# Attention on one Trainium2 core: four scores and two maxima tiles in one stretch a step, weighted sums one step behind

## What is computed

```python
scores = jnp.einsum('bqhd,bkhd->bhqk', Q, K) / np.sqrt(HEAD_DIM)      # 16 wide heads
scores = scores + slopes[None, :, None, None] * rel[None, None, :, :]
attn = jax.nn.softmax(scores, axis=-1)
out = jnp.einsum('bhqk,bkhd->bqhd', attn, V).reshape(bsz, seq_len, EMBED_DIM)
```

## Time and profile before

| | us |
|---|---|
| time before, median of 3 runs | 5108.2 |
| lowest and highest of the runs | 5095.89 and 5113.9 |
| span of the profiled execution | 5138.9 |
| of it the attention's loop, from the trace | 337 to 2909 |
| PE, DVE, ACT busy in that loop | 2556.23, 2502.93, 2248.42 |

### The profile page before, as it was taken

How to read it: one execution, slowest core, us unless ns; L and a number is a source line. 1 busy time by engine, 2 the same in 40 slices (tenths; PEclk the granted TensorE clock), 3 DMA queues, 4 the chain that set the end, 5 groups by cost and what they waited for, 6 DMA issues and landing times. The chain is left out here.

```text
span 5138.9 us, 109366 instructions
## 1 busy us (share of the span) xinstructions
PE 4706.1 (92%) x35413; PEld 2589.8 (50%) x35413; DVE 4275.5 (83%) x6882; ACT 3471.8 (68%) x6677; POOL 1377.0 (27%) x1279
## 2 busy tenths in 40 slices
PE   5869999999999999999999689999599999955998
PEld 4723333333333333333333267777366666645887
DVE  5779999999999999999999768878677877775554
ACT  2428888888888888888888523223377877734554
POOL 1111111111111111111111133333234443435776
PEclk8969999999999999999999889999699999956999
DMA  4931222212222122221222211111100000044442
GB/s 153 349 67 35 52 52 46 43 35 53 52 46 43 35 53 51 46 43 38 50 54 43 71 40 37 41 45 37 53 21 27 25 23 28 21 156 164 166 160 92
DMA packets 236717, 340.13 MB, mean 66 GB/s; under 512 B 60215, under 2 KB 170034, under 8 KB 227612
## 3 DMA queue, kind: packets, MB, share of 16 engines
q1 hardware_dynamic: 220032, 275.39, 22.3%
q0 software_dynamic: 16192, 58.43, 3.1%
HBM read 205.62 MB, written 136.18 MB: 67 GB/s over the span
## 5 line engine op out<-in xcount | busy, mean ns | idle before, releaser
L719 DVE TENSOR_REDUCE at_mxp<-at_ps_m 128x2 f32<-128x1024 f32 x2092 | 2524.4, 1221 | 70.2 <-PE at_ps_m L772 47.3
L692 ACT ACTIVATE at_prob<-at_ps_s 128x512 f32<-128x512 f32 x4100 | 2227.3, 596 | 323.5 <-PE at_ps_s L762 299.7
L782 PE MATMUL at_ps_o<-at_prob,at_vs 128*32 128x256 f32 x16384 | 1313.1, 392 | 13.9 <-ACT at_osum L698 13.9
L762 PE MATMUL at_ps_s<-at_qs,at_ks 51*128 51x512 f32 x4100 | 1036.7, 500 | 2.7 <-ACT at_prob L692 2.7
L772 PE MATMUL at_ps_m<-at_ks,at_qs 49*128 49x512 f32 x4184 | 859.0, 406 | 49.8 <-DMA at_ks<-t_alibi 34.4
L762 PEld LDWEIGHTS at_ps_s<-at_qs,at_ks 51*128 51x128 f32 x4100 | 384.6, 183 | 853.3 <-ACT at_prob L692 852.8
L782 PEld LDWEIGHTS at_ps_o<-at_prob,at_vs 128*32 128x32 f32 x16384 | 322.9, 108 | 778.2 <-issue 389.7
L564 POOL TENSOR_TENSOR at_total<-at_total,at_minus 128x16 f32<-128x16 f32 x65 | 189.6, 2917 | 1128.4 <-DMA at_total<-at_osum 1128.4
L772 PEld LDWEIGHTS at_ps_m<-at_ks,at_qs 49*128 49x128 f32 x4184 | 403.7, 190 | 73.7 <-DVE at_mxp L719 38.0
L67 DVE TENSOR_TENSOR ex_hidc<-ex_hid,ex_hidc 128x512 fp32r<-128x512 f32 x128 | 158.5, 1250 | 169.6 <-ACT ex_hid L2550 169.6
L1222 PE MATMUL mi_ps_f<-mi_w,mi_act 128*128 128x256 f32 x1024 | 260.1, 399 | 17.4 <-DVE mi_acc L1072 17.1
(11 more groups left out here) (317 smaller groups left out, 6161.6 us busy)
## 6 DMA issues: line engine op xcount, KB each, us to landing
t_parts<-pr_parts SPq DMA_DIRECT2D x64, 512.0 KB, 6.4
ex_w<-in_fw SPq DMA_DIRECT2D x32, 1024.0 KB, 7.4
at_ks<-t_parts SPq DMA_DIRECT2D x102, 256.0 KB
t_buf<-at_blank POOLq DMA_DIRECT2D x64, 384.5 KB, 3.2
at_qs<-t_parts SPq DMA_DIRECT2D x96, 256.0 KB
at_vs<-t_v SPq DMA_DIRECT2D x17, 1024.0 KB, 4.8
ex_rest<-t_buf SPq DMA_DIRECT2D x16, 1026.0 KB, 5.2
t_v<-pr_vaug SPq DMA_DIRECT2D x64, 256.0 KB, 5.6
```

The lines of the kernel that those rows point to most:

```text
L692: nc.scalar.activation(prob[0 if up is None else (t + 1) % 2][:, j, :], ps_s[bank][:, :], ACT.Exp).then_inc(s_read, 1)
L719: nc.vector.tensor_reduce(out[:, s4, k + i, 2 * pair:2 * pair + 2], ps_m[i][:, :, :], AX.X, ALU.max).then_inc(mx_read, 1)
L762: nc.tensor.matmul(ps_s[bank][:, :], ks[s][a:a + QROWS, j // 2, t1 * P:(t1 + 1) * P], qs[s][a:a + QROWS, j // 2, c * T:(c + 1) * T], start ...
L782: last = nc.tensor.matmul(ps_o[32 * j:32 * j + 32, q0:q1], vs[s][:, t, 32 * j:32 * j + 32], prob[t % 2][:, j, q0:q1], start=(t == 0 and ha ...
```

## The change

In the new order a step has one row-tiled stretch and one column-tiled stretch: scores 0 and 1, maxima tile 0, score 2, score 3, maxima tile 1, and then all four weighted sums at once, for all 512 queries, with the probabilities of the step before. The scores are shifted by one head: a chunk's step t holds heads 1, 2 and 3 of its own step and head 0 of the next (`head`). `at_prob` has four tiles in place of two. The copy of a chunk's sums moves behind the four exponentials of the next chunk's first step, and PE's waits for it and for the new values (`v_in`) to that chunk's second step; the wait for the next chunk's maxima moves from before score 0 of the last step to before its score 3. Before the loop one score stands in place of four, behind two more memsets on POOL (a slice of `at_vs` and one `at_prob` tile), and the first weighted sum works on those ones; behind the loop one weighted sum is added. The two matmuls of a maxima tile change places. The number of PSUM banks of the scores is still 3.

```diff
+        PROBS = 4
+        prob = [sb(f"prob{r}", [P, HPG, T]) for r in range(PROBS)]
...
+        AHEAD = RING + 1
...
             if up is None:
-                return j, bank_of(LOOP - HPG + j), 0
+                return 0, bank_of(LOOP - 1), 0
             back = next(a for a in range(1, LOOP) if bank_of((k - a) % LOOP) == bank_of(k))
-            return HPG + up * LOOP + k, bank_of(k), back
+            return 1 + up * LOOP + k, bank_of(k), back
+        def head(t, j):
+            return (t, j + 1) if j < HPG - 1 else (t + 1, 0)
...
+                nc.gpsimd.memset(vs[1][:, KT - 1, :], 1.0)
+                nc.gpsimd.memset(prob[PROBS - 1][:, :, :], 1.0).then_inc(before_first, 1)
...
                 act.wait_ge(always, 1)
-                for j in range(HPG):
-                    exponentials(None, 0, 0, j)
+                act.sem_inc(s_read, AHEAD)
+                exponentials(None, 0, 0, 0)
                 with loop(nc, act, 0, TURNS) as up:
                     for r in range(CH):
-                        take_sums(up * CH + r)
                         for t in range(KT):
                             for j in range(HPG):
                                 exponentials(up, r, t, j)
+                            if t == 0:
+                                take_sums(up * CH + r)
...
-                    if up is not None or j >= RING:
-                        pe.wait_ge(s_read, i - (back or RING) + 1)
+                    if up is not None:
+                        pe.wait_ge(s_read, AHEAD + i - back + 1)
...
-                    for a in range(2):
+                    for a in (1, 0):
                         last = nc.tensor.matmul(ps_m[i][:, a, :], qs[s][a * 64:a * 64 + MXR, pair, q0:q0 + P],
...
-                def weighted(up, r, s, t, half):
-                    q0, q1 = half * T // 2, (half + 1) * T // 2
-                    if half == 0:
-                        pe.wait_ge(s_read, HPG + up * LOOP + (r * KT + t) * HPG)
+                def weighted(up, r, s, t, steps):
+                    pe.wait_ge(s_read, AHEAD + 1 + up * LOOP + steps * HPG)
                     for j in range(HPG):
-                        last = nc.tensor.matmul(ps_o[32 * j:32 * j + 32, q0:q1], vs[s][:, t, 32 * j:32 * j + 32], prob[t % 2][:, j, q0:q1],
+                        last = nc.tensor.matmul(ps_o[32 * j:32 * j + 32, :], vs[s][:, t, 32 * j:32 * j + 32], prob[t % PROBS][:, j, :],
...
+                            scores(up, r, t, 0, s, c, t)
+                            scores(up, r, t, 1, s, c, t)
+                            max_scores(*best, 0)
+                            scores(up, r, t, 2, s, c, t)
                             if t + 1 == KT:
                                 pe.wait_ge(max_in, 16 * HPG * (n + 2))
-                            scores(up, r, t, 0, *nxt)
-                            scores(up, r, t, 1, *nxt)
-                            max_scores(*best, 0)
-                            if t == 0:
+                            scores(up, r, t, 3, *nxt)
+                            max_scores(*best, 1)
+                            if t == 1:
                                 pe.wait_ge(o_out, n + 1)
...
-                            weighted(up, r, s, t, 0)
-                            scores(up, r, t, 2, *nxt)
-                            scores(up, r, t, 3, *nxt)
-                            max_scores(*best, 1)
-                            weighted(up, r, s, t, 1)
+                            weighted(up, r, s if t or c else 1 - s, (t - 1) % KT, r * KT + t)
+                weighted(TURNS, 0, (TURNS * LU - 1) % 2, KT - 1, 0)
```

More of the change, by code:

```diff
@@ L499, in attend_phase @@
         vs = [sb(f"vs{s}", [P, KT, HPG * 32]) for s in range(2)]
-        prob = [sb(f"prob{r}", [P, HPG, T]) for r in range(2)]
+        PROBS = 4
+        prob = [sb(f"prob{r}", [P, HPG, T]) for r in range(PROBS)]
         mxp = [sb(f"mxp{r}", [P, SUB, MXS, HPG]) for r in range(2)]
@@ L521, in attend_phase @@
         norm_done, max_in, always, cleared = sem("norm_done"), sem("max_in"), sem("always"), sem("cleared")
+        before_first, sums_set = sem("before_first"), sem("sums_set")
         o_stored = [sem(f"o_stored{r}") for r in range(2)]
@@ L538, in bank_of @@
             return (k + (LOOP % RING == 1 and k >= LOOP // 2)) % RING
+        AHEAD = RING + 1
+        assert KT % PROBS == 0
         def place(up, n, t, j):
@@ L690, in exponentials @@
                     i, bank, _ = place(up, n, t, j)
+                    step, k = (0, 0) if up is None else head(t, j)
                     act.wait_ge(s_done, i + 1)
-                    nc.scalar.activation(prob[0 if up is None else (t + 1) % 2][:, j, :], ps_s[bank][:, :], ACT.Exp).then_inc(s_read, 1)
+                    nc.scalar.activation(prob[step % PROBS][:, k, :], ps_s[bank][:, :], ACT.Exp).then_inc(s_read, 1)
                 def take_sums(n):
                     act.wait_ge(norm_done, n)
-                    act.wait_ge(o_done, n)
+                    act.wait_ge(o_done, n + 1)
                     nc.scalar.copy(osum[:, :], ps_o[:, :]).then_inc(o_out, 1)
                 act.wait_ge(always, 1)
-                for j in range(HPG):
-                    exponentials(None, 0, 0, j)
+                act.sem_inc(s_read, AHEAD)
+                exponentials(None, 0, 0, 0)
                 with loop(nc, act, 0, TURNS) as up:
                     for r in range(CH):
-                        take_sums(up * CH + r)
                         for t in range(KT):
@@ L735, in _ @@
                 nc.vector.memset(ks[0][32:64, :, :].bitcast(F32), 1.0).then_inc(ones_set[0], 1)
-                nc.vector.memset(ps_o[:, :], 1.0)
-                dve.drain()
-                dve.sem_inc(always, 1)
+                nc.vector.memset(ps_o[:, :], 1.0).then_inc(sums_set, 1)
                 for t in range(LEAD):
@@ L757, in scores @@
                 def scores(up, n, t, j, s, c, t1):
-                    a = j % 2 * 64
+                    k = 0 if up is None else head(t, j)[1]
+                    a = k % 2 * 64
                     i, bank, back = place(up, n, t, j)
-                    if up is not None or j >= RING:
-                        pe.wait_ge(s_read, i - (back or RING) + 1)
-                    nc.tensor.matmul(ps_s[bank][:, :], ks[s][a:a + QROWS, j // 2, t1 * P:(t1 + 1) * P],
-                                     qs[s][a:a + QROWS, j // 2, c * T:(c + 1) * T], start=True, stop=True).then_inc(s_done, 1)
+                    if up is not None:
+                        pe.wait_ge(s_read, AHEAD + i - back + 1)
+                    nc.tensor.matmul(ps_s[bank][:, :], ks[s][a:a + QROWS, k // 2, t1 * P:(t1 + 1) * P],
+                                     qs[s][a:a + QROWS, k // 2, c * T:(c + 1) * T], start=True, stop=True).then_inc(s_done, 1)
                 def max_scores(n, s, c, t, i):
@@ L774, in max_scores @@
                     last.then_inc(mx_done, 1)
-                def weighted(up, r, s, t, half):
-                    q0, q1 = half * T // 2, (half + 1) * T // 2
-                    if half == 0:
-                        pe.wait_ge(s_read, HPG + up * LOOP + (r * KT + t) * HPG)
+                def weighted(up, r, s, t, steps):
+                    pe.wait_ge(s_read, AHEAD + 1 + up * LOOP + steps * HPG)
                     for j in range(HPG):
-                        last = nc.tensor.matmul(ps_o[32 * j:32 * j + 32, q0:q1], vs[s][:, t, 32 * j:32 * j + 32], prob[t % 2][:, j, q0:q1],
-                                                start=(t == 0 and half == 0), stop=(t == KT - 1), tile_position=(0, 32 * j), skip_group_check=True)
-                    if half and t + 1 == KT:
+                        last = nc.tensor.matmul(ps_o[32 * j:32 * j + 32, :], vs[s][:, t, 32 * j:32 * j + 32], prob[t % PROBS][:, j, :],
+                                                start=(t == 0), stop=(t == KT - 1), tile_position=(0, 32 * j), skip_group_check=True)
+                    if t + 1 == KT:
                         last.then_inc(o_done, 1)
@@ L794, in _ @@
                 pe.wait_ge(max_in, 16 * HPG)
-                for j in range(HPG):
-                    scores(None, 0, 0, j, 0, 0, 0)
+                pe.wait_ge(before_first, 1)
+                pe.wait_ge(sums_set, 1)
+                scores(None, 0, 0, 0, 0, 0, 0)
                 with loop(nc, pe, 0, TURNS) as up:
```

## The result

The changed kernel takes 5461.97 us (median of four runs, 5450.53 to 5477.15) against 5111.05 (four runs, 5095.89 to 5132.02): a ratio of 1.0678, interval 1.0632 to 1.0725. Its profiled execution took 5457.84 us.

The account below looks back on a forecast made before the run. PE's order was taken to set the step before; afterwards a chain through score 3's bank wait, 2.86 us against 2.48, gives +389, the copy -16: 5108.2 + 373 = 5481 us, range 5410 to 5600.

Parts of the forecast that it names:

- PE's own order: Attention loop before the change: PE's sequence of matmuls sets the step of 2.48 us, with DVE close behind at 2.26.
- Score 3 waits for score 0's exponential: Merged stretch: PE could reach score 3 after 0.58 us, but its bank is free after 1.19; about 0.6 us standing still.
- The terms of the chain: New step: score to exponential 0.54, exponential 0.60, release 0.05, score 3 to sums 0.67, sums 1.00; 2.86 us.
- the unknown term: Weighted sums up to the next score 0: 1.00 us if the second half costs only streaming, at most 1.14.
- Rival 3: Attention loop: the chain is shorter, say by 0.37 us of overlap, and meets the old step; 5092 to 5120; chance 0.02.
- The copy of the sums: Each chunk: PE's 0.30 us wait goes, the copy delays the exponential by 0.05; -16 us in all.
- Rival 1: Attention loop: the bank's wait doesn't bind, DVE's reductions set a step of 2.26 us; faster, 4867 us; chance 0.05.
- Rival 2: Attention loop: PE's pauses lower its clock; 4.50 us a step, 7160 us throughout or 5650 for a tenth; chance 0.05.
- Busy shares: Loop after the change: PE 93% busy, DVE and ACT busy as long as before, about 1000 weight-load waits for an exponential.
- changes of kind: PE's switches between maxima and sums matmuls: some 0.12 us each, two of four saved, 0.24 a step, not setting the end.

Follow-up runs that it names:

- run 3: Exponentials taken over 256 of the 512 columns, on the kernel before the change; half of the exponentials left out: 5105.75 us.
- run 2: Exponentials taken over 256 of the 512 columns, on the changed kernel; half of the exponentials left out: 5247.29 us.
- run 4: Changed kernel with the fourth score of each step and its exponential left out, three score banks kept: 4981.09 us.
- run 5: Changed kernel with four score banks, the maxima getting three single banks in place of two double ones: 5585.19 us, ratio 1.0873 to the kernel before.
- run 1: Changed kernel with the second maxima tile moved ahead of score 3, all work kept: 5229.03 us, ratio 1.0208 to the kernel before.

## Why the prediction was right, step by step

- **PE's own order sets the step before.** Shown by run 3: shorter exponentials change nothing there.
- **Score 3 waits for score 0's exponential.** Shown from three sides: a shorter exponential shortens the step by as much (run 2), without reuse the wait is gone (run 4), with a fourth bank score 3 goes at 0.58 us (run 5, the prediction's own figure for PE by itself). Measured 1.18 us after score 0, predicted 1.19.
- **The terms of the chain:** 0.53 (predicted 0.54), 0.65 (0.60 + 0.05), 0.67 (0.67), 0.99 (1.00). The sums were the unknown term, between 1.00 and 1.14, and the lower end was right: the second half cost no more than its streaming. The step is 2.84 in place of 2.86, as the first and the last term were each read a hundredth too long: 1024 x 0.02 = 20 us. That this is just the distance to the forecast is partly chance. The prediction had nothing for the loop's two ends: the first chunk, which begins at half clock, was 10.4 us longer than the median chunk before (50.34 against 39.99), where the clock fell once more, and 3.9 after (49.43 against 45.54), and the last chunk after is 1.9 shorter (43.62). These 8 us less are made up for by 3 us of the copy (below) and by 5 of the 351 that lie outside the loop, which is within the spread of the runs.
- **Rival 3, a shorter chain.** The terms follow one another without overlap: their sum, 0.53 + 0.65 + 0.67 + 0.99, is the step of 2.84. Run 1 changed one term, 0.67 to 0.43, and the step lost just about that, 2.84 to 2.62.
- **The copy of the sums.** PE's wait for it is gone. Its delay to the exponentials was taken as 0.05 and is 0.09: in this timeline the score at 1522.53 has its exponential at 1523.15, 0.62 later in place of 0.53.

```profile
1522.53 0.50 PE L774 MATMUL at_ps_s<-at_qs,at_ks 51*128 51x512 f32 x2
...
1522.66 0.59 ACT L710 COPY at_osum<-at_ps_o 128x512 f32<-128x512 f32 x1 [0.37 <-PE at_ps_o L792]
...
1523.15 2.07 ACT L704 ACTIVATE at_prob<-at_ps_s 128x512 f32<-128x512 f32 x4
```

That is 64 x 0.04 = 3 us the other way. Putting the copy elsewhere by itself wasn't tried, nor was changing the order of a tile's two maxima matmuls; the terms leave no time in the step for the latter.
- **Rival 1, DVE's pace.** It doesn't occur in the changed kernel. Run 4, which comes nearest to it and leaves out a quarter of the scores, took 4981 us, not 4867: 32 reductions of 1.13 us are 36.2 a chunk, but with DVE's other work a chunk took 37.56, 64 x 1.4 = 90 us more; the other 24 are not taken apart. The Trainium skill (TensorEngine Tiling (Array Packing), Performance Considerations, PSUM Bottleneck) says that tiling speeds up TensorE but not the evacuation of PSUM, which may become the bottleneck. Run 4 agrees, with DVE 98% busy and no bank of the scores reused within a stretch. In the changed kernel ACT (73% busy in the loop) and DVE (85%) had throughput to spare, and the time a bank takes to come back set the step.
- **Rival 2, the clock.** PE pauses in every step (0.23 us in the records), and the granted clock was 1.00 over the loop, its first steps apart. The Trainium skill (TensorE: Matmul & The Clock Gate, A second HAM failure mode: psum-queue depth-cycling) describes a clock that swings where PE idles briefly between groups of matmuls. Such swings did not come here. The rival's price can be read all the same, since the loop's first steps ran at half clock, 0.50 in the window from 329 to 344: score 0 at 334.49 and the next at 338.99, 4.50 us, as priced.

```profile
334.49 0.79 PE L774 MATMUL at_ps_s<-at_qs,at_ks 51*128 51x512 f32 x2
...
338.99 0.80 PE L774 MATMUL at_ps_s<-at_qs,at_ks 51*128 51x512 f32 x2
```

- **Busy shares.** DVE and PE came out as forecast (PE 92% of the loop, forecast 93%; 1021 waits of the scores, forecast about 1000; the weight loads' 2042 count score 0's too, which only follows the sums). ACT "busy as before" held in work, not in records.

## What to carry to other kernels

Before merging two stretches of matmuls, count how often one stretch writes each PSUM buffer. In this kernel, once there were more writes than buffers, the time from a matmul through its reader and back (1.18 us through ACT, about 1.2 through DVE in run 5) lay on the path, though the readers were not full, and moving a bank from one user to another only moved the wait. If a reuse can't be avoided, put every instruction that doesn't need it ahead of the waiting one in its queue, as run 1 does, and keep other work between the two uses, as the kernel before does. The two changes of kind that the merge saved, by the prediction's estimate 0.12 us each, were worth less than this one wait, some 0.6 us a step.

## What the runs showed that I had not expected

PE's busy share can hide a wait. In run 1 PE is busy 2394.20 of 2400 us by the windows, though score 3 waits for ACT in every step; the record of the matmuls ahead of it (0.61 us for two) runs into the wait:

```profile
400.00:2800.00 2400.00, 2394.20 (x14696) 931.70 (x14688) 2184.86 (x2012) 1923.97 (x3731) 287.77 (x230) 1.00 0.23 43
```

What gives it away is the weight load's own wait (0.42 us for ACT) and DVE and ACT idle for PE at once. And half of the columns cost more than half: in run 5 four reductions of 512 columns took 2.48 us and a record of one is 0.68 long, so back to back one comes every (2.48 - 0.68)/3 = 0.60 us, where one of 1024 comes every 1.13. An exponential over 256 columns releases PE 0.44 us after its start (run 2), one over 512 after 0.65.
